# One loop per compute engine for all eight rounds, first round included, and whole-quad transfers at both ends of a gathered two-step residual matmul

## The chip, the cores and the metric

The kernel runs on one core of one Trainium2 chip. The metric is the device time of the program in microseconds (us), the median of several runs. TensorE has two clock levels, 1.2 and 2.4 GHz; the profile gives the granted one as a share of full speed (1.00 or 0.50).

## What is computed

```
x  = x + einsum('bct,bcd->bdt', x, W0[i_b])            # i_b = itok_B_1_198[b], 200 matrices of 128x128
x  = x + einsum('bct,bcd->bdt', x, W1[j_b]) + bias[j_b] # j_b = itok_B_0_7[b], 8 matrices of 128x128
# x: 128 batches b, 128 channels c, 1024 points t, float32
```

Both steps are linear in x, so the kernel forms one 128x128 matrix per batch and applies it once: with J = I + W1[j_b], the matrix is M = W0[i_b] J + J, and the output of the batch is M^T x + bias.

## The kernel before

x and out lie in memory as 32 quads of four batches (128 channels x 4 batches x 1024 points, 2 MB each). The ring `xy` in SBUF holds eight pairs of batches (slots 0 to 7), that is four quads; results are written over x in the same slot and stored from there. A round is one turn of the ring, 16 batches, and there are eight rounds.

For each batch the 64 KB matrix of W0 is loaded into its own place in `w0_home`. A batch whose index already occurred earlier uses the place of the first batch with that index (its home) and its load is skipped by a condition; homes are worked out on the chip by DVE and PE at the start (L353 to L367) from the 128 index words. Round 0 can't know them yet, so its 16 matrices are loaded without a condition and read from `w0_home` in place.

Per pair of batches (slot s):

- POOL: `pick` (L231) waits for the W0 matrices of the slot, reads two words per batch (home and j) from `pick_words`, and copies W0 to `w0_pick` and J to `j_pick`. Before that it waits until the quad that held the slot in the round before has been stored (L276). In round 0 `pick_first` (L248) copies J alone.
- PE: `product` (L281) makes W0 J of both batches in PSUM; `results` (L295) makes M^T x of one batch, as two halves of 512 points. The program order puts `product` of the next pair between the two batches of this pair, in every pair, also across the border between two rounds: the loop over rounds (L330) begins with the last pair of the round before. Round 0 stands unrolled ahead of the loop (L321 to L329), the last pair behind it.
- DVE: `sum_m` (L370) adds J to the product and gives M; `left` (L378) adds the bias to the left half and writes it to `xy`. Seven rounds are a loop, the eighth is written out.
- ACT: `right` (L400) does the right half. Seven rounds loop, one is written out.

SP issues every transfer but three, in program order. At the start: W1 with bias, both pairs of quad 0 (1 MB each), then for each quad its four W0 loads and the x load of the next quad (L176 to L184). Then three unrolled stretches, and a loop over rounds 1 to 6 (L203): for each quad the four W0 loads of the next quad, the store of the quad three back, and, once that slot's former contents are stored, the x load of this quad. SP reads index and condition of the W0 loads from `load_words`, two words per batch, in one read of eight words (L123).

The end (L211 to L227): the last quad of x is loaded as one pair (1 MB) and four pieces of 256 KB, each with a semaphore of its own; its second pair is stored as four pieces, two from SP (L225) and two from ACT (L421), each issued as soon as its half has been written.

```
            for k in range(PAIR):
                for h in range(2):
                    sp.dma_start(xy[:, LAST, k, half(h)], x[NQ - 1, :, QB - PAIR + k, half(h)])\
                      .then_inc(last_x_loaded[2 * k + h], 16)
```

Of the kernel before, what the change touches and what calls it, by code (L numbers as in the profile page):

```python
# [11 lines left out]
def conditioned_residual_kernel(nc, x, cond, w0_t, w1_bias, out):  # L12
# [12 lines left out]
    B = NQ * QB  # L25
# [16 lines left out]
    assert QUADS == 4 and QUAD == 2 and PAIRS % RING == 0 and HALF <= 512 and RING % MB == 0 and ROUND_B % YB == 0  # L42

    with ExitStack() as ctx:
# [16 lines left out]
        load_words = sb("load_words", [1, B, 2], I32)  # L61
        cond_words = sb("cond_words", [1, 2, B], I32)
        pick_words = sb("pick_words", [1, B, 2], I32)
# [21 lines left out]
        pair_loaded = [sem(f"pair_loaded{s}") for s in range(QUAD)]  # L85
# [3 lines left out]
        last_x_loaded = [sem(f"last_x_loaded{n}") for n in range(2 * PAIR)]  # L89
        last_stored = sem("last_stored")  # L90
# [25 lines left out]

        block = ctx.enter_context(nc.Block())

        @block.sync
        def _(sp):  # L120
            def words_of(words):

                return nc.values_load_multi_w_load_instructions(  # L123
                    words, engines=(mybir.EngineType.SP,), min_val=0, max_val=N0 - 1,
                    skip_runtime_bounds_check_because="the reference indexes a table of N0 rows with each cond word, "
                                                      "and each word of need is 0 or 1")[1]
# [6 lines left out]
            def load_w0_first(q):  # L133
                words = words_of(cond_words[0:1, 0, q * QB:(q + 1) * QB])
                for k in range(QB):
                    load_one(q * QB + k, q * QUAD + k // PAIR, words[k], None)

            def load_w0(r, s, pairs=1):

                for n in range(s, s + pairs):  # L140
                    sp.wait_ge(w0_loaded[n], r * (PAIR * 16))
                b = r * ROUND_B + s * PAIR
                words = words_of(load_words[0:1, bass.ds(b, pairs * PAIR), :].rearrange("o b f -> o (b f)"))
                for k in range(pairs * PAIR):
                    load_one(b + k, s + k // PAIR, words[2 * k], words[2 * k + 1])
# [7 lines left out]
            def wait_out(r, s):  # L153
                for k in range(PAIR):
                    b = s * PAIR + k
                    sp.wait_ge(left_out[b % YB], r * (ROUND_B // YB) + (b // YB + 1))  # L156
                    sp.wait_ge(right_out[b % YB], r * (ROUND_B // YB) + (b // YB + 1))
# [29 lines left out]
            sp.wait_ge(home_ready, 4)  # L187
# [39 lines left out]
            sp.wait_ge(last_stored, 2 * PAIR * 16)  # L227

        @block.gpsimd
        def _(pool):  # L230
            def pick(r, s):  # L231


                pool.wait_ge(w0_loaded[s], r * (PAIR * 16) + PAIR * 16)
                _, words = nc.values_load_multi_w_load_instructions(
                    pick_words[0:1, bass.ds(r * ROUND_B + s * PAIR, PAIR), :].rearrange("o b f -> o (b f)"),
                    engines=(mybir.EngineType.Pool,),
                    skip_runtime_bounds_check_because="each word is checked against its own range below")
                for k in range(PAIR):
                    home = nc.s_assert_within(words[2 * k], 0, B - 1)  # L240
                    i = nc.s_assert_within(words[2 * k + 1], 0, N1 - 1)
                    nc.gpsimd.tensor_copy(w0_pick[:, s, k, :],  # L242
                                          w0_home[:, bass.ds(home, 1), :].rearrange("k b c -> k (b c)"))
                    last = nc.gpsimd.tensor_copy(  # L244
                        j_pick[:, s, k, :], j_all[:, bass.ds(i, 1), :].rearrange("c n d -> c (n d)"))
                last.then_inc(picked, 1)

            def pick_first(s):  # L248


                _, words = nc.values_load_multi_w_load_instructions(
                    cond_words[0:1, 1, s * PAIR:(s + 1) * PAIR], engines=(mybir.EngineType.Pool,),
                    skip_runtime_bounds_check_because="each word is checked against its own range below")
                for k in range(PAIR):
                    i = nc.s_assert_within(words[k], 0, N1 - 1)
                    last = nc.gpsimd.tensor_copy(  # L256
                        j_pick[:, s, k, :], j_all[:, bass.ds(i, 1), :].rearrange("c n d -> c (n d)"))
                last.then_inc(picked, 1)

            nc.gpsimd.memset(ones[:], 1.0).then_inc(ones_ready, 1)  # L260
# [8 lines left out]
            for s in range(RING):  # L269
                pick_first(s)  # L270

            pool.wait_ge(home_ready, 4)
            with pool.Fori(1, ROUNDS) as r:
                for s in range(RING):

                    pool.wait_ge(stored[s // QUAD], stored_once(r, s // QUAD))  # L276
                    pick(r, s)

        @block.tensor
        def _(pe):  # L280
            def product(r, s, first=False):  # L281

                pe.wait_ge(picked, r * RING + (s + 1))
                if first:
                    pe.wait_ge(w0_loaded[s], PAIR * 16)
                if not first or s >= MB:

                    pe.wait_ge(m_ready[s % MB], r * (RING // MB) + s // MB)
                for k in range(PAIR):
                    w0_of_k = w0_home[:, s * PAIR + k, :] if first else w0_pick[:, s, k, :]  # L290
                    last = nc.tensor.matmul(m_ps[:, s % MB, k * D:(k + 1) * D], w0_of_k,  # L291
                                            j_pick[:, s, k, 0:D], start=True, stop=True)
                last.then_inc(product_ready, 1)

            def results(r, s, k, first=False, last=False):  # L295

                b = s * PAIR + k
                if k == 0:
                    if first and s < QUAD:
                        pe.wait_ge(pair_loaded[s], 16)  # L300
                    elif not last:
                        pe.wait_ge(x_loaded[s // QUAD], r * 16 + (16 if s >= QUAD else 0))
                    pe.wait_ge(m_ready[s % MB], r * (RING // MB) + (s // MB + 1))
                for h in range(2):
                    if last:
                        pe.wait_ge(last_x_loaded[2 * k + h], 16)
                    if not first or b >= YB:

                        pe.wait_ge((left_out, right_out)[h][b % YB], r * (ROUND_B // YB) + b // YB)
# [11 lines left out]
            product(0, 0, first=True)  # L321
# [16 lines left out]
            for k in range(PAIR):  # L338
                results(ROUNDS - 1, LAST, k, last=True)

        @block.vector
        def _(dve):

            dve.wait_ge(cond_loaded, 16)
            nc.vector.tensor_copy(cond0_row[:], cond_words[:, 0, :]).then_inc(cond0_row_ready, 1)  # L345
            dve.wait_ge(w1_loaded, 16)
            dve.wait_ge(eye_ready, 1)
            nc.vector.tensor_tensor(j_all[:, :, 0:D], j_all[:, :, 0:D],  # L348
                                    eye[:].rearrange("c (o d) -> c o d", o=1).to_broadcast([C, N1, D]), ALU.add)\
              .then_inc(j_ready, 1)  # L350
# [11 lines left out]
            nc.vector.tensor_copy(load_words[:, :, 0], cond_words[:, 0, :]).then_inc(home_ready, 1)  # L362
# [87 lines left out]
```

## Time and profile before

| | |
|---|---|
| median of 3 runs | 342.62 us (342.51 to 342.78) |
| profiled execution: own time | 343.0 us |
| profiled execution: span, first to last instruction | 341.2 us |
| PE busy | 272.9 us (80%) |
| DVE, ACT, POOL busy | 126.3, 97.0, 65.8 us |
| HBM read, written | 76.03 MB, 67.11 MB |
| mean granted clock | 0.952 |

Busy time is the sum of an engine's instructions; a busy share of PE isn't PE at its peak. DMA share in the stretches below is the mean over the core's 16 DMA engines, so 0.06 is one engine of 16 at work; it can read a few hundredths over 1. "To landing" is the time from a transfer's issue to the last of its completion signals.

### The profile page before, as it was taken

The page shows a single profiled execution, that of the slowest core. Times are in us where ns is not written, and L with a number is a line of the kernel's source. Part 1 is how long each engine was busy: PE and PEld are TensorE (multiplying, and loading weights), DVE is VectorE, ACT ScalarE, POOL GpSimd, SP SyncE. Part 2 cuts the span into 40 slices and gives each one's busy share as a digit, 9 for nine tenths or more (in the row PEclk, how much of TensorE's full clock was granted, in tenths as well). Part 3 has the DMA queues.
Part 4 walks back from the last instruction along what each step waited for, and adds up shares of the span by engine and source line. Part 5 has one row for each costly group of instructions (what it writes and reads, how often), then busy time and mean ns, then how long its engine had stood idle before and what let it go on. Part 6 is the DMA issues. An engine that isn't in the chain of part 4 may idle for free.

```text
span 341.2 us, 4867 instructions
## 1 busy us (share of the span) xinstructions
PE 272.9 (80%) x774; PEld 131.8 (39%) x774; DVE 126.3 (37%) x202; ACT 97.0 (28%) x135; POOL 65.8 (19%) x249
## 2 busy tenths in 40 slices
PE   1799997678777798786997977889697987978980
PEld 1355443334333354343443433444343443434430
DVE  3145543343333334243442433434243432424440
ACT  1033352232322224132241324313143321323330
POOL 2400311131122211222111222121222111222000
PEclk9999999999999979799897999979799997989996
DMA  7999999999999999999999999999999999999993
GB/s 304 417 409 396 422 430 419 413 423 421 432 434 423 426 422 414 431 424 423 427 427 423 431 430 426 427 421 426 433 426 430 427 429 426 425 426 424 413 387 137
DMA packets 24058, 140.80 MB, mean 413 GB/s; under 512 B 2673, under 2 KB 14322, under 8 KB 15474
## 3 DMA queue, kind: packets, MB, share of 16 engines
q1 hardware_dynamic: 23760, 140.20, 98.7%
q10 hardware_dynamic: 290, 0.53, 0.4%
q14 instruction: 7, 0.06, 0.0%
q8 instruction: 1, 0.02, 0.0%
HBM read 76.03 MB, written 67.11 MB: 419 GB/s over the span
## 4 chain that ended last, share of the span: by engine, by line
DMA 61%; SPq 16%; PE 13%; issue 7%; ACT 0%; DVE 0%; DVEq 0%
DMA out<-xy 54%; PE y_ps L310 11%; SPq L129 9%; SPq L123 5%; DMA xy<-x 4%; DMA w_home<-w_t 2%; PE m_ps L291 2%; SPq L148 2%; ACT xy L406 0%; SPq L162 0%; SPq L151 0%; SPq L203 0%; SPq L156 0%; PE home_ps L324 0%; SPq L176 0%
## 5 line engine op out<-in xcount | busy, mean ns | idle before, releaser
L310 PE MATMUL y_ps<-xy,m_sb 128*128 128x512 f32 x512 | 251.4, 627 | 49.2 <-DMA xy<-x 48.2
L310 PEld LDWEIGHTS y_ps<-xy,m_sb 128*128 128x128 f32 x512 | 94.6, 200 | 155.1 <-issue 155.1
L406 ACT ACTIVATE xy<-y_ps,j_pick 128x512 f32<-128x512 f32 x128 | 88.0, 687 | 227.4 <-PE y_ps L310 227.4
L382 DVE TENSOR_SCALAR xy<-y_ps,j_pick 128x512 f32<-128x512 f32 x128 | 96.1, 751 | 147.9 <-PE y_ps L310 147.9
L242 POOL COPY w_pick<-w_home 128x128 f32 x112 | 33.2, 296 | 238.3 <-issue 238.3
L291 PEld LDWEIGHTS m_ps<-j_pick,w_pick 128*128 128x128 f32 x224 | 35.7, 200 | 30.2 <-issue 29.7
L374 DVE TENSOR_TENSOR m_sb<-m_ps,j_pick 128x256 f32<-128x256 f32 x64 | 27.2, 425 | 47.7 <-PE m_ps L291 46.1
L291 PE MATMUL m_ps<-j_pick,w_pick 128*128 128x128 f32 x224 | 34.9, 279 | 0.0
L244 POOL COPY j_pick<-j_all 128x129 f32 x112 | 33.4, 298 | 0.1
L291 PE MATMUL m_ps<-j_pick,w_home 128*128 128x128 f32 x32 | 5.9, 315 | 6.6 <-DMA w_home<-w_t 6.6
L406 ACT ACT_TABLE_LOAD x7 | 9.0, 1283 | 7.5 <-POOL j_pick L256 7.4
L291 PEld LDWEIGHTS m_ps<-j_pick,w_home 128*128 128x128 f32 x32 | 5.7, 225 | 10.6 <-POOL j_pick L256 7.2
L256 POOL COPY j_pick<-j_all 128x129 f32 x16 | 4.8, 298 | 9.9 <-issue 9.5
L316 PE MATMUL cond_ps<-cond_row,ones 1*128 1x128 f32 x2 | 0.8, 482 | 2.4 <-DVE cond_row L345 2.4
L365 DVE TENSOR_TENSOR load_words<-home_ps,batch_less_b 1x128 int32<-1x128 f32 x1 | 0.3, 280 | 5.0 <-PE home_ps L324 5.0
L348 DVE TENSOR_TENSOR j_all<-j_all,eye 128x1024 f32<-128x1024 f32 x1 | 1.2, 1226 | 1.9 <-DMA j_all<-w_bias 1.9
L316 PEld LDWEIGHTS cond_ps<-cond_row,ones 1*128 1x128 f32 x2 | 0.5, 305 | 2.4 <-issue 2.4
L345 DVE CAST cond_row<-cond_words 1x128 f32<-1x128 int32 x1 | 0.2, 215 | 2.1 <-DMA cond_words<-cond 2.1
L324 PE MATMUL home_ps<-eye,home_less_b 128*1 128x128 f32 x2 | 0.6, 394 | 0.0
L317 PEld LDWEIGHTS cond_ps<-ones,cond_row 1*128 1x128 f32 x2 | 0.5, 328 | 0.0
L317 PE MATMUL cond_ps<-ones,cond_row 1*128 1x1 f32 x2 | 0.4, 277 | 0.0
L355 DVE TENSOR_SCALAR same<-cond_ps,cond_col 128x128 f32<-128x128 f32 x1 | 0.4, 351 | 0.0
(16 smaller groups left out, 2.8 us busy)
## 6 DMA issues: line engine op xcount, KB each, us to landing
xy<-x SPq DMA_DIRECT2D x30, 2048.0 KB, 15.1
out<-xy SPq DMA_DIRECT2D x29, 2048.0 KB, 15.0
w_home<-w_t SPq DMA_DIRECT2D x128, 64.0 KB
out<-xy SPq DMA_DIRECT2D x5, 1024.0 KB, 9.7
xy<-x SPq DMA_DIRECT2D x3, 1024.0 KB, 7.7
xy<-x SPq DMA_DIRECT2D x4, 256.0 KB, 13.4
j_all<-w_bias SPq DMA_DIRECT2D x1, 516.0 KB, 3.4
out<-xy SPq DMA_DIRECT2D x2, 256.0 KB, 4.7
```

Of the source, the lines that this page charges most:

```text
L123: return nc.values_load_multi_w_load_instructions(words, engines=(mybir.EngineType.SP,), min_val=0, max_val=N0 - 1, skip_runtime_bounds_ch ...
L129: sp.dma_start(w0_home[:, bass.ds(b, 1), :].rearrange("k b c -> k (b c)"), w0_t[bass.ds(i, 1), :, :].rearrange("n k c -> (n k) c"), cond=n ...
L148: sp.dma_start(slots(q), quad_of(x, r, q)).then_inc(x_loaded[q], 16)
L242: nc.gpsimd.tensor_copy(w0_pick[:, s, k, :], w0_home[:, bass.ds(home, 1), :].rearrange("k b c -> k (b c)"))
L244: last = nc.gpsimd.tensor_copy(j_pick[:, s, k, :], j_all[:, bass.ds(i, 1), :].rearrange("c n d -> c (n d)"))
L256: last = nc.gpsimd.tensor_copy(j_pick[:, s, k, :], j_all[:, bass.ds(i, 1), :].rearrange("c n d -> c (n d)"))
L291: last = nc.tensor.matmul(m_ps[:, s % MB, k * D:(k + 1) * D], w0_of_k, j_pick[:, s, k, 0:D], start=True, stop=True)
L310: nc.tensor.matmul(y_ps[:, b % YB, h, :], m_sb[:, s, k, :], xy[:, s, k, half(h)], start=True, stop=True).then_inc(y_ready, 1)
L316: nc.tensor.matmul(cond0_ps[:, 0:B], ones[:], cond0_row[:], start=True, stop=True)
L374: nc.vector.tensor_tensor(m_sb[:, s, :, :], m_ps[:, s % MB, 0:PAIR * D].rearrange("c (k d) -> c k d", k=PAIR), j_pick[:, s, :, 0:D], ALU.a ...
L382: nc.vector.tensor_scalar(xy[:, s, k, half(0)], y_ps[:, b % YB, 0, :], j_pick[:, s, k, D:D + 1], None, ALU.add).then_inc(left_out[b % YB], 1)
L406: nc.scalar.activation(xy[:, s, k, half(1)], y_ps[:, b % YB, 1, :], ACT.Identity, bias=j_pick[:, s, k, D:D + 1]).then_inc(right_out[b % YB ...
```

## The change

What it does:

- Each of PE, DVE, ACT and POOL runs one loop of eight rounds; nothing is unrolled before or behind it. At the border of two rounds `product` of slot 0 now follows the last batch of the round before, it is no longer put between that pair's two batches.
- Round 0 is like the others: POOL picks W0 and J for it too, and so waits for the homes (`home_ready`) before its first copy. POOL works by quads (`pick_quad`): one read of four j words and one of four home words, then for each pair two J copies, the wait for W0, two W0 copies. It waits for the results of the round before in these slots, not for their store.
- `load_words` and `pick_words`, two words per batch, are gone. SP reads the index words as they came (`cond_words`) and the condition from `need_words`, two reads of four words; every word has its range stated where it is read, so the separate range instructions go.
- DVE makes the homes before it adds I to W1; `ones` is set by DVE, not POOL. `left_out` and `right_out` begin at 8, so that the first round waits by the same formula.
- Start: pair 1 of quad 0 is issued behind the four W0 loads of quad 0, and each later quad's x load ahead of its W0 loads.
- End: the last x quad is one load of 2 MB, and the second pair of the last quad is stored as one transfer of 1 MB by SP once all four halves are written. SP alone waits for the stores.
- The instructions of all engines take 55 KB, not 85.

```diff
@@ SP @@
-            for s in range(QUAD):
-                load_pair(0, s, pair_loaded[s])
+            load_pair(0, 0, x_loaded[0])
             sp.wait_ge(cond_loaded, 16)
-            for q in range(QUADS):
+            load_w0_first(0)
+            load_pair(0, 1, x_loaded[0])
+            for q in range(1, QUADS):
+                load_quad(0, q)
                 load_w0_first(q)
-                if q < QUADS - 1:
-                    load_quad(0, q + 1)
...
             store_quad(ROUNDS - 1, 0)
-            sp.wait_ge(stored[QUADS - 1], stored_once(ROUNDS - 1, QUADS - 1))
-            load_pair(NQ - 1, LAST - 1, x_loaded[QUADS - 1])
-            for k in range(PAIR):
-                for h in range(2):
-                    sp.dma_start(xy[:, LAST, k, half(h)], x[NQ - 1, :, QB - PAIR + k, half(h)])\
-                      .then_inc(last_x_loaded[2 * k + h], 16)
+            load_quad_again(ROUNDS - 1, QUADS - 1)
             for q in range(1, QUADS - 1):
                 store_quad(ROUNDS - 1, q)
             store_pair(ROUNDS - 1, LAST - 1)
-            for k in range(PAIR):
...
-                b = LAST * PAIR + k
-                sp.wait_ge(left_out[b % YB], (ROUNDS - 1) * (ROUND_B // YB) + b // YB + 1)
-                sp.dma_start(out[NQ - 1, :, QB - PAIR + k, half(0)], xy[:, LAST, k, half(0)]).then_inc(last_stored, 16)
...
+            store_pair(ROUNDS - 1, LAST)
...
@@ POOL @@
+            def pick_quad(r, q):
...
+                pool.wait_ge(left_out[YB - 1], pick_free(r, q * QUAD + QUAD - 1))
+                pool.wait_ge(right_out[YB - 1], pick_free(r, q * QUAD + QUAD - 1))
+                for p in range(QUAD):
+                    s = q * QUAD + p
+                    for k in range(PAIR):
+                        nc.gpsimd.tensor_copy(
+                            j_pick[:, s, k, :],
+                            j_all[:, bass.ds(j_of[p * PAIR + k], 1), :].rearrange("c n d -> c (n d)"))
...
+                    pool.wait_ge(w0_loaded[s], r * (PAIR * 16) + PAIR * 16)
...
-            for s in range(RING):
-                pick_first(s)
...
-            pool.wait_ge(home_ready, 4)
-            with pool.Fori(1, ROUNDS) as r:
-                for s in range(RING):
...
-                    pool.wait_ge(stored[s // QUAD], stored_once(r, s // QUAD))
-                    pick(r, s)
+            pool.wait_ge(home_ready, 2)
+            with pool.Fori(0, ROUNDS) as r:
+                for q in range(QUADS):
+                    pick_quad(r, q)
@@ PE @@
-            product(0, 0, first=True)
...
-            for s in range(1, RING):
-                results(0, s - 1, 0, first=True)
-                product(0, s, first=True)
-                results(0, s - 1, 1, first=True)
-            with pe.Fori(1, ROUNDS) as r:
-                results(r - 1, LAST, 0)
+            with pe.Fori(0, ROUNDS) as r:
                 product(r, 0)
-                results(r - 1, LAST, 1)
-                for s in range(1, RING):
-                    results(r, s - 1, 0)
-                    product(r, s)
-                    results(r, s - 1, 1)
-            for k in range(PAIR):
-                results(ROUNDS - 1, LAST, k, last=True)
+                for s in range(RING):
+                    results(r, s, 0)
+                    if s < LAST:
+                        product(r, s + 1)
+                    results(r, s, 1)
@@ ACT @@
-            for k in range(PAIR):
-                b = LAST * PAIR + k
-                right(ROUNDS - 1, LAST, k)
-                act.wait_ge(right_out[b % YB], (ROUNDS - 1) * (ROUND_B // YB) + b // YB + 1)
-                act.dma_start(out[NQ - 1, :, QB - PAIR + k, half(1)], xy[:, LAST, k, half(1)]).then_inc(last_stored, 16)
```

How it moves instructions, at the places that the prediction speaks of. First PE's first instructions, before (x is `xy`, the matrix M is `m_sb`):

```order
L317 MATMUL cond_ps<-ones,cond_row 128x1
L291 MATMUL m_ps<-j_pick,w_home 128x128 [waits w0_loaded0,picked]
L291 MATMUL m_ps<-j_pick,w_home 128x128
L324 MATMUL home_ps<-eye,home_less_b 1x128 [waits home_step,eye_ready]
L310 MATMUL y_ps<-xy,m_sb 128x512 [waits m_ready0,pair_loaded0]
```

and with the change:

```order
L315 MATMUL cond_ps<-ones,cond_row 128x1
L321 MATMUL home_ps<-eye,home_less_b 1x128 [waits home_step,eye_ready]
L323 UNCONDITIONAL_BRANCH
L323 ISA
L294 MATMUL m_ps<-j_pick,w_pick 128x128 [waits picked]
L294 MATMUL m_ps<-j_pick,w_pick 128x128
```

The homes' last step on PE (`home_ps`) stood behind the first product and its wait for W0; now it stands ahead of it.

Second, the transfers that SP issues at the end, before:

```order
L162 DMA out<-xy 128x4096 [waits left_out1,right_out1,right_out0,left_out0]
L151 DMA xy<-x 128x2048 [waits stored3]
L216 DMA xy<-x 128x512 x4
L162 DMA out<-xy 128x4096 [waits left_out1,right_out1,right_out0,left_out0] x2
L166 DMA out<-xy 128x2048 [waits left_out1,right_out1,right_out0,left_out0]
L225 DMA out<-xy 128x512 [waits left_out0]
L225 DMA out<-xy 128x512 [waits left_out1]
L44 UNCONDITIONAL_BRANCH [waits last_stored]
```

and with the change:

```order
L185 DMA out<-xy 128x4096 [waits left_out1,right_out1,right_out0,left_out0]
L171 DMA xy<-x 128x4096 [waits stored3]
L185 DMA out<-xy 128x4096 [waits left_out1,right_out1,right_out0,left_out0] x2
L189 DMA out<-xy 128x2048 [waits left_out1,right_out1,right_out0,left_out0] x2
L45 UNCONDITIONAL_BRANCH [waits stored2,stored3,stored1,stored0]
```

The last quad comes in as one transfer and its second pair goes out as one.

## Rows read from the trace of the kernel before

**Rows 1.** The profile page: span, and DMA share in 40 slices.
```profile
span 341.2 us, 4867 instructions
...
DMA  7999999999999999999999999999999999999993
```

**Rows 2.** Busy time by stretch: start and length, engines, clock, DMA share, GB/s.
```profile
core 0: us, PE busy (x) PEld busy (x) DVE busy (x) ACT busy (x) POOL busy (x), PEclk, DMA share, GB/s
...
240.00:300.00 60.00, 49.91 (x139) 23.56 (x138) 22.53 (x36) 17.10 (x24) 12.85 (x48) 0.94 1.01 428
...
324.00:325.00 1.00, 1.00 (x4) 0.45 (x3) 0.29 (x1) 0.09 (x1) 0.00 (x0) 1.00 0.22 90
325.00:330.00 5.00, 5.00 (x16) 2.47 (x15) 2.38 (x4) 1.87 (x3) 0.00 (x0) 1.00 1.01 428
330.00:335.00 5.00, 1.12 (x3) 0.19 (x1) 0.75 (x1) 0.88 (x2) 0.00 (x0) 1.00 1.00 397
336.00:337.00 1.00, 0.00 (x0) 0.00 (x0) 0.00 (x0) 0.00 (x0) 0.00 (x0) 0.50 0.12 47
...
339.00:340.00 1.00, 0.00 (x0) 0.00 (x0) 0.00 (x0) 0.00 (x0) 0.00 (x0) 0.50 0.06 25
```

**Rows 3.** Who waited for whom, all engines, then SP's queue: us in total, times, longest.
```profile
PE y_ps L310 <- DMA xy<-x: 48.2, 27, 3.0
...
SPq L44 <- DMA out<-xy: 9.4, 1, 9.4
```

**Rows 4.** Transfers to landing: SP's L216, SP's last L225, ACT's last L421.
```profile
L216 SPq DMA_DIRECT2D xy<-x x4: 521/660/770, 310.7 to 312.7; - x4
...
DMA to landing us min/median/max: 13.3/13.4/13.4
...
L225 SPq DMA_DIRECT2D out<-xy x1: 332/332/332, 331.1 to 331.1; - x1
...
DMA to landing us min/median/max: 4.5/4.5/4.5
...
L421 ACTq DMA_DIRECT2D out<-xy x1: 338/338/338, 331.9 to 331.9; - x1
...
DMA to landing us min/median/max: 8.9/8.9/8.9
```

**Rows 5.** Timeline of the last quads: start us, us, engine, line, what, idle before.
```profile
304.83 3.62 PE L310 MATMUL y_ps<-xy,m_sb 128*128 128x512 f32 x4 [2.43 <-DMA xy<-x]
...
323.57 1.95 PE L310 MATMUL y_ps<-xy,m_sb 128*128 128x512 f32 x4 [0.21 <-DMA xy<-x]
...
331.16 0.69 ACT L406 ACTIVATE xy<-y_ps,j_pick 128x512 f32<-128x512 f32 x1 [0.97 <-PE y_ps L310]
```

**Rows 6.** Stretch of the slow matmuls of rows 5, columns as in rows 2.
```profile
304.80:308.20 3.40, 3.37 (x4) 1.52 (x5) 0.75 (x1) 0.00 (x0) 0.00 (x0) 0.50 1.02 439
```

**Rows 7.** Timeline of the start.
```profile
2.88 2.16 SPq L129 DMA_DIRECT2D w_home<-w_t  x4
...
5.30 0.15 DVE L353 COPY cond_col<-cond_ps 128x1 f32<-128x1 f32 x1
...
6.65 0.66 POOL L256 COPY j_pick<-j_all 128x129 f32 x2 [4.80 <-issue]
...
10.04 1.19 PE L291 MATMUL m_ps<-j_pick,w_home 128*128 128x128 f32 x4 [6.61 <-DMA w_home<-w_t]
...
12.73 3.75 PE L310 MATMUL y_ps<-xy,m_sb 128*128 128x512 f32 x4 [0.99 <-DVE m_sb L374]
```

**Rows 8.** Timeline of PE across a border of two rounds.
```profile
80.08 3.60 PE L310 MATMUL y_ps<-xy,m_sb 128*128 128x512 f32 x8
```

**Rows 9.** DMA queues: packets, MB, share of 16 engines.
```profile
q1 hardware_dynamic: 23760, 140.20, 98.7%
q10 hardware_dynamic: 290, 0.53, 0.4%
q14 instruction: 7, 0.06, 0.0%
```

More of the change, by code:

```diff
@@ L120, in _, with words_of, index_words @@
         def _(sp):
-            def words_of(words):
+            def words_of(words, last, why):
                 return nc.values_load_multi_w_load_instructions(
-                    words, engines=(mybir.EngineType.SP,), min_val=0, max_val=N0 - 1,
-                    skip_runtime_bounds_check_because="the reference indexes a table of N0 rows with each cond word, "
-                                                      "and each word of need is 0 or 1")[1]
+                    words, engines=(mybir.EngineType.SP,), min_val=0, max_val=last,
+                    skip_runtime_bounds_check_because=why)[1]
+            def index_words(b):
+                return words_of(cond_words[0:1, 0, b], N0 - 1,
+                                "the reference indexes a table of N0 rows with each of these cond words")
             def load_one(b, s, i, needed):
@@ L229, in _ @@
+            sp.wait_ge(stored[QUADS - 1], stored_once(ROUNDS, QUADS - 1) + 16)
         @block.gpsimd
         def _(pool):
[L231 to L238, printed above, removed]
-                for k in range(PAIR):
[L240 to L253, printed above, removed]
-                for k in range(PAIR):
[L255 to L258, printed above, removed]
@@ L260, in _, with words_of @@
-            nc.gpsimd.memset(ones[:], 1.0).then_inc(ones_ready, 1)
+            def words_of(words, last, why):
+                return nc.values_load_multi_w_load_instructions(
+                    words, engines=(mybir.EngineType.Pool,), min_val=0, max_val=last,
+                    skip_runtime_bounds_check_because=why)[1]
+            def pick_quad(r, q):
+                b = bass.ds(r * ROUND_B + q * QB, QB)
+                j_of = words_of(cond_words[0:1, 1, b], N1 - 1,
+                                "the reference indexes a table of N1 rows with each of these cond words")
+                home_of = words_of(home_words[0:1, b], B - 1,
+                                   "a home is the number of the first batch with the same w0, so it is below B")
+                pool.wait_ge(left_out[YB - 1], pick_free(r, q * QUAD + QUAD - 1))
[7 more added lines that the diff above has]
+                    pool.wait_ge(w0_loaded[s], r * (PAIR * 16) + PAIR * 16)
+                    for k in range(PAIR):
+                        last = nc.gpsimd.tensor_copy(
+                            w0_pick[:, s, k, :],
+                            w0_home[:, bass.ds(home_of[p * PAIR + k], 1), :].rearrange("k b c -> k (b c)"))
+                    last.then_inc(picked, 1)
@@ L279, in _, with product @@
         @block.tensor
         def _(pe):
-            def product(r, s, first=False):
+            def product(r, s):
                 pe.wait_ge(picked, r * RING + (s + 1))
[L284 to L288, printed above, removed]
                 for k in range(PAIR):
-                    w0_of_k = w0_home[:, s * PAIR + k, :] if first else w0_pick[:, s, k, :]
-                    last = nc.tensor.matmul(m_ps[:, s % MB, k * D:(k + 1) * D], w0_of_k,
+                    last = nc.tensor.matmul(m_ps[:, s % MB, k * D:(k + 1) * D], w0_pick[:, s, k, :],
@@ L292, in product, with results @@
                                             j_pick[:, s, k, 0:D], start=True, stop=True)
                 last.then_inc(product_ready, 1)
-            def results(r, s, k, first=False, last=False):
+            def results(r, s, k):
                 b = s * PAIR + k
                 if k == 0:
[L299 to L303, printed above, removed]
+                    if s % QUAD == 0:
+                        pe.wait_ge(x_loaded[s // QUAD], x_loaded_once(r, s // QUAD))
+                    pe.wait_ge(m_ready[s % MB], m_made(r, s))
@@ L304, in results @@
                 for h in range(2):
[L305 to L309, printed above, removed]
+                    pe.wait_ge((left_out, right_out)[h][b % YB], y_free(r, b))
                     nc.tensor.matmul(y_ps[:, b % YB, h, :], m_sb[:, s, k, :], xy[:, s, k, half(h)],
```

80 lines of the change are left out of this document (41 added, 39 removed).

## The prediction

> **What bounds the kernel now.** I read the page's row of the DMA share first, since 140 MB in 341 us is a lot for one core: it stands at nine tenths or more from the second slice to the last but one [rows 1]. The stretches say the same in numbers: from 240 to 300 us the 16 DMA engines are busy all the time (share 1.01) and move 428 GB/s, while PE, the busiest compute engine, works 49.91 of 60 us [rows 2]. PE waited 27 times for x, 48.2 us in all, 1.8 us a time [rows 3]. So the transfers set the pace in the middle, and a change on a compute engine there counts only if it makes the DMA engines run dry.
>
> Then the end, in three views. The stretches show a hole from 324 to 325 us (share 0.22): SP's store of quad 2 was issued at 324.2, behind the results of that quad, and nearly everything ahead of it had gone. From 325 the share is full again until 335, and then falls to 0.12 and at last to 0.06, one engine of 16, at 25 GB/s [rows 2]. The landings tell who that is: SP's last piece, issued at 331.1, landed 4.5 us later at 335.6; ACT's last piece, issued at 331.9, landed 8.9 us later, at 340.8 [rows 4], and SP ended its wait for it then [rows 3]. The two are alike in size, so one DMA engine is some 5 us behind the other 15, and the span ends with its queue, not with the last result (ACT done at 331.85) [rows 5].
>
> That queue can be added up. The last piece of x, issued at 312.7, was complete after 13.4 us, at 326.1 [rows 4]. Behind it lie three stores' worth of results: quads 1 and 2 (2 MB each) and the two pairs of quad 3 (1 MB each), 6.29 million bytes, 0.393 million per engine. At 428/16 = 26.75 GB/s per engine [rows 2] that is 14.7 us, and 326.1 + 14.7 = **340.8**, just the landing. The late engine has thus no hole at all, not even at 324 to 325; it is the resource that bounds the kernel to its last microsecond.
>
> The Trainium skill (DMA: Bandwidth & Descriptors, Latency and other measured facts) says that two of the 16 engines are usually slower, and guesses at rings that only software-made descriptors use. Here all data go through hardware queues [rows 9] and an engine is late all the same, so the guess doesn't carry to this case. By that guess the end would be set by the 15 others; that is a rival below.
>
> **The change, part by part.** The sum is made against the profiled execution, 343.0 us of its own time (span 341.2, 1.8 around it); the median of the runs is 342.62, 0.4 below.
>
> *The end.* The same bytes are left when x is complete: the load of quad 3 is 2 MB either way, and it ends in the same place of the queue, so all of it is there at about 326.0. What changes is who may begin. Before, PE began on pair 0 of this quad at 323.57 [rows 5], when the first megabyte had come; now it must wait for 2 MB, 2.4 us more. Its work on the two pairs took from 323.57 to 331.16, 7.6 us, so now 326.1 + 7.6 = 333.7. But PE will have been idle for some 2.7 us ahead of it (it finished quad 2 about 0.2 before 323.57). At 304.83, behind an idle time of 2.43 us, four matmuls took 3.62 us [rows 5] at a granted clock of 0.50, that is 1.2 GHz [rows 6], where the four at 323.57, behind 0.21 us of idle time, took 1.95 [rows 5]. I add the difference, 1.7 us: 335.4, with ACT's 0.7 us 336.1, and SP issues the last megabyte at **336.2**. From issue to the first bytes I take 1.0 us, from the hole: issued at 324.2, share full again from 325 [rows 2]. The data start at 337.2. The late engine reaches this megabyte at 340.8 less 1/16 MB at 26.75 GB/s (2.45 us), at **338.4**. So the store is there 1.2 us before its turn, and costs nothing. The 15 others are idle in between but need only 337.2 + 2.45 = 339.7, also before 340.8. Without this cover (no late engine) the compute tail would show. In return the pieces' rows of 2 KB become rows of 8 and 16 KB. No row prices that; the sum above fits to 0.1 us with one rate for both, so the gain lies between 0 and 0.3, and I take 0.1. SP's last waits are four where it waited for one semaphore and ACT for four: 0 to 0.4 us, taken as 0.1 since all but one are long met.
>
> *The start.* SP issues pair 1 behind four W0 loads, which took 2.16 us [rows 7], so at about 4.7 us and not at 1.7. The 0.5 MB of W1 and 1 MB of pair 0, issued before, last to about 6 us, and the four W0 loads stand between: the engines don't run dry. Bounds 0 and 0.5 us, taken 0. The homes come sooner: DVE's first step of them no longer stands behind the addition to W1 (`cond_col` at 5.30), PE's last no longer behind the wait for W0 (10.04) [rows 7]. They should be ready at 6.5 and not at 12.3; POOL adds two reads of words and two W0 copies per pair (a pair of copies is 0.66 us), so the first product comes at 9.5 to 10 and the first `y_ps` at about 11, not 12.73 [rows 7]. That lets stores be issued up to 1.7 us earlier, into a queue that is full in this time [rows 1]: worth nothing, bounds 0 and -1.7.
>
> *The middle.* SP reads 4 + 4 words for 8, and drops the range instructions; it issues the same transfers in the same order. POOL's picks wait for less (results, not stores). PE's product of slot 0 now stands alone between two rounds, as does DVE's sum: product 0.6 and sum 0.4 us, no longer overlapped, 1.2 us with the way between, eight times. It falls into the time in which PE waits for the next x, 1.8 us a time [rows 3], so 0. If that cover were gone, it would be 9 us. In the last quad there is no such border.
>
> *The code.* 30 KB less to fetch. The trace shows 7 packets, 0.06 MB, of instruction fetch in the span [rows 9], on the same DMA engines. All 30 KB on the late engine would be 30 KB at 26.75 GB/s, 1.1 us; spread over 16, under 0.1. I take 0.1.
>
> **Sum:** -0.1 (rows) + 0.1 (waits) + 0 + 0 + 0 - 0.1 (code) = -0.1 us: 342.9 for a profiled execution, and **342.5** against the median 342.62. No change, then: under 0.2% (0.7 us), which is about the least that a measurement of this kernel can tell from none.
>
> **The rivals.**
> 1. *The last store comes too late (slower).* Place: PE's last quad. It decides from 337.4 on: an issue later than that misses the late engine's turn at 338.4, and each microsecond more is one on the end. For it: only 1.2 us of margin, and a quad wholly at 1.2 GHz costs 16 matmuls and 2 products at twice the time, some 14 to 15 us for 7.6, so issue at 341.5 and an end of 345, about +4. Against it: the low stretch at 304.8 ended within 3.4 us, four matmuls [rows 5, 6]. Half way is 344.5. Chance 0.12.
> 2. *Stalls at the loops' ends (slower).* The Trainium skill (Runtime: NRT & Kernel Launch, Instruction fetch mechanics) says that a taken branch whose target is outside the two fetched pages stalls the engine for a DMA fetch, and advises full unrolling; that speaks against this change. As a mechanism here: one stall on each of PE, DVE, ACT and POOL at every border of rounds, in a DMA queue some 10 us deep for a newly issued packet (transfers land 13 us after issue [rows 4]), 10 us a round in the worst case, 2 us of it hidden. Against it: PE crossed such a border in eight matmuls that took 3.60 us without a gap [rows 8]. Should it show once or twice only, where a larger body no longer fits, the time would be 344 to 346. Chance 0.04.
> 3. *The fetches lay on the late engine (faster).* Then up to 1.1 us go: 341.5. For it: something makes one engine late, and fetches are small transfers to few engines. Against: 7 packets in 341 us explain at most 2 us of 5. Chance 0.14.
> 4. *The late engine isn't late after the change,* as the guess on software rings would have it. Then the end is 339.7 + 0.4, about 1 us less: 341.5. Every full run of before speaks against it. Chance 0.03.
> 5. *The earlier first result is passed on,* so that the change's new order of the start does pay: 342.6 - 1.7 = 340.9. The full DMA share speaks against it. Chance 0.02.
>
> **How the numbers follow.** The forecast (within 0.7 us of 342.62) has 0.65; rivals 3 to 5 make faster 0.19, rivals 1 and 2 slower 0.16. The range takes in rival 3, the lower bounds of the code and of the rows (-1.1, -0.3) and above the bounds of waits and start (+0.4, +0.5) and the first third of rival 1: 341.3 to 344.0.
>
> **What the profile after should show.** DMA share full to about 331, then a partial hole up to 333 (the 15 engines wait for the store of the next to last pair), another near 336, and one engine alone to 340.7. PE's first matmul of the last quad at 326, slow; last ACT at 335.4 to 336; SP's last store issued near 336 and landed near 340.7. First `y_ps` at 11 us. No idle time on PE for x shorter than 1 us at a round's border. Wrong would be: the last store landing 3.5 us after its issue with 16 engines alike (then compute set the end), or a hole in the DMA share at a border of rounds.

## The result: 0.4% slower, and the profile after

| | before | changed |
|---|---|---|
| median | 342.62 us (7 runs, 342.15 to 343.08) | 343.98 us (7 runs, 342.56 to 344.91) |
| ratio, with its 95% interval | | 1.0038 [1.0021, 1.0056] |
| profiled execution, own time | 343.0 us | 342.56 us |

The forecast was 342.5 us: no change, to within 0.2%. The measured median is 1.36 us above the kernel before, and the interval excludes both no difference and 0.2%. The runs also spread more than before: 2.35 us between the fastest and the slowest, where the kernel before shows 0.93. (Over the whole study 4 of the 94 executions of the kernel before took over 343.5 us, one of them 346.28, and 23 of the 31 with pair 1 behind four W0 loads.) And the profiled execution is the fastest of the seven. A reader who compares two pages alone would call this change slightly faster. One profile isn't enough here.

The whole of it looks like the one before: DMA share and end [rows 1], PE's wait for x and SP's last wait [rows 3]:

```profile
span 340.8 us, 4236 instructions
...
DMA  8999999999999999999999999999999999999975
```

```profile
PE y_ps L308 <- DMA xy<-x: 45.2, 25, 3.0
...
SPq L243 <- DMA out<-xy: 4.9, 1, 4.9
```

The end, by stretches with the columns of [rows 2]: the partial hole that was 324 to 325 us is now longer, then the share is nearly full to 337, 0.36 from 337 to 338, and then one engine alone is at work to 340:

```profile
325.00:330.00 5.00, 4.90 (x15) 2.27 (x14) 2.44 (x4) 1.51 (x3) 0.00 (x0) 1.00 0.69 292
330.00:335.00 5.00, 3.26 (x8) 1.14 (x6) 1.50 (x2) 1.92 (x3) 0.00 (x0) 1.00 0.93 388
...
339.00:340.00 1.00, 0.00 (x0) 0.00 (x0) 0.00 (x0) 0.00 (x0) 0.00 (x0) 0.50 0.04 16
```

The last store, SP's L189, with its landing (it answers to the last pieces in [rows 4]), and PE's and ACT's last work [rows 5]:

```profile
L189 SPq DMA_DIRECT2D out<-xy x1: 332/332/332, 334.1 to 334.1; - x1
...
DMA to landing us min/median/max: 6.2/6.2/6.2
```

```profile
315.87 3.56 PE L308 MATMUL y_ps<-xy,m_sb 128*128 128x512 f32 x4 [2.59 <-DMA xy<-x]
...
327.94 5.32 PE L308 MATMUL y_ps<-xy,m_sb 128*128 128x512 f32 x12
```

A megabyte alone on 16 engines needs 1.0 + 2.45 us by the forecast's own rows; this one took 6.2, to 340.3. So here too the last store stood in the queue of one late engine, and the results were there in time. That reading holds in every profile of the study: the last landing of all came 14.8 to 15.4 us after the last piece of x was complete, whether the last store had been issued 6.0 us after that (the kernel before) or 8.6 (every kernel with the changed end). The forecast's sum for this queue was 14.7.

The start [rows 7] is where something new stands. SP's queue and then PE:

```profile
1.21 0.43 SPq L174 DMA_DIRECT2D xy<-x  x1
2.80 1.97 SPq L150 DMA_DIRECT2D w_home<-w_t  x4
4.82 0.43 SPq L174 DMA_DIRECT2D xy<-x  x1
```

```profile
8.85 1.22 PE L294 MATMUL m_ps<-j_pick,w_pick 128*128 128x128 f32 x4 [3.42 <-POOL w_pick L270]
11.30 3.77 PE L308 MATMUL y_ps<-xy,m_sb 128*128 128x512 f32 x4 [1.23 <-DMA xy<-x]
```

The first result came at 11.3 us and not at 12.73, as forecast. But the stretch from 6 to 9 us moved less than before. First the kernel before, then the changed one:

```profile
6.00:9.00 3.00, 0.00 (x0) 0.00 (x0) 0.71 (x4) 1.28 (x1) 1.19 (x4) 1.00 0.99 401
```

```profile
6.00:9.00 3.00, 0.15 (x1) 0.15 (x1) 0.22 (x2) 0.11 (x1) 1.20 (x6) 1.00 1.06 352
```

49 GB/s less for 3 us are 0.15 MB, 0.3 us at 428 GB/s: little, but this is the fastest execution. The first experiment's profile shows what the others look like.

One correction to the list of the change further up: the sequence of the later x and W0 transfers at the start is the same in both kernels (W0 of quad 0, x of quad 1, W0 of quad 1, and so on). Only pair 1 moved, from ahead of the W0 loads of quad 0 to behind them.

### The profile page after: what moved, and what is told of

Its sections match the earlier page's. It is cut to its first block, busy times and chain, and to the rows that moved or that the text cites. A ratio compares the mean times of both kernels' runs of the same rounds, so it can differ in the third digit from the quotient of the medians.

```text
span 340.8 us, 4236 instructions
## 1 busy us (share of the span) xinstructions
PE 278.6 (82%) x774; PEld 135.8 (40%) x774; DVE 126.2 (37%) x201; ACT 98.2 (29%) x136; POOL 64.9 (19%) x264
## 4 chain that ended last, share of the span: by engine, by line
DMA 64%; SPq 18%; PE 11%; issue 5%; ACT 1%
DMA out<-xy 50%; DMA xy<-x 13%; SPq L150 10%; PE y_ps L308 10%; SPq L141 5%; SPq L171 2%; PE m_ps L294 1%; ACT xy L395 1%; DMA cond_words<-cond 0%; SPq L185 0%; SPq L179 0%; SPq L226 0%; SPq L174 0%; SPq L180 0%; SPq L189 0%
## 5 line engine op out<-in xcount | busy, mean ns | idle before, releaser
L270 POOL COPY w_pick<-w_home 128x128 f32 x128 | 33.9, 293 | 204.7 <-DMA w_home<-w_t 204.7
L294 PEld LDWEIGHTS m_ps<-j_pick,w_pick 128*128 128x128 f32 x256 | 44.1, 217 | 40.0 <-issue 33.7
L294 PE MATMUL m_ps<-j_pick,w_pick 128*128 128x128 f32 x256 | 43.8, 299 | 3.4 <-POOL w_pick L270 3.4
L264 POOL COPY j_pick<-j_all 128x129 f32 x128 | 34.0, 295 | 36.7 <-issue 23.5
## 6 DMA issues: line engine op xcount, KB each, us to landing
out<-xy SPq DMA_DIRECT2D x29, 2048.0 KB, 15.4
```

The source lines that it names most:

```text
L264: nc.gpsimd.tensor_copy(j_pick[:, s, k, :], j_all[:, bass.ds(j_of[p * PAIR + k], 1), :].rearrange("c n d -> c (n d)"))
L270: last = nc.gpsimd.tensor_copy(w0_pick[:, s, k, :], w0_home[:, bass.ds(home_of[p * PAIR + k], 1), :].rearrange("k b c -> k (b c)"))
```

## Experiments

Two theories were set against each other. **T**, the forecast's first rival in its widest form: the coarser end leaves too little cover. **S**: at the start the DMA engines run short, because pair 1 is queued too late, and time lost by the late engine can't be won back. A third possibility, the loops and picks, had to be told apart from both.

### 1. The changed kernel again

No edit. 

> The changed kernel once more. Its first runs spread from 342.56 to 344.91 us, where the kernel before spread 0.9 us. Theory T (the tail: the last whole-quad load and whole-pair store leave too little cover, and which run is slow is decided by where TensorE's low-clock stretch falls): +1.0 to +1.6 us over the kernel before, spread of 2 us, and a profile in which the last store's issue or the late DMA engine's landing of it is late. Theory S (the start: pair 1 behind the W0 loads): the same time, but the excess is there by 30 us.

Measured: 343.64 us, 12 runs (342.64 to 344.61), ratio 1.0022 [1.0008, 1.0036]. The profiled execution took 344.14. Its start:

```profile
6.00:9.00 3.00, 0.21 (x1) 0.21 (x2) 0.15 (x1) 0.17 (x1) 1.26 (x6) 1.00 0.87 255
```

255 GB/s where the kernel before has 401: 0.44 MB less, 1.0 us at full rate, and a DMA share of 0.87, so engines stood idle and others moved slowly. SP issued pair 1 at 4.7, and this transfer landed 7.1 us later:

```profile
L174 SPq DMA_DIRECT2D xy<-x x1: 424/424/424, 4.7 to 4.7; - x1
...
DMA to landing us min/median/max: 7.1/7.1/7.1
```

At 11.8, then, where pair 1 landed at 9.4 in the kernel before (issued at 1.7, 7.7 us to landing).

The trace also lists every packet with its size, and the size tells what it belongs to: 512 bytes is a row of W0, 8 KB a row of a pair. In the kernel before, pair 1's first packet starts at 6.12 us, as pair 0's last does at 6.08, and takes 0.31 us like the others; the W0 rows come at 8.46 to 9.82. Here the W0 rows come at 5.93 to 7.38. Pair 1's first packet starts at 6.97, 2.2 us after its issue, its first 16 packets take 0.60 us each on the average, and its last packet starts at 11.2 and not at 8.8. So the loss has two parts, engines without work and slow first packets. The end of this execution had wide holes for 15 engines (332 to 333: share 0.09; 335.5 to 336.5: 0.07), yet the last store still landed 6.2 us after its issue at 335.7:

```profile
339.50:340.50 1.00, 0.00 (x0) 0.00 (x0) 0.00 (x0) 0.00 (x0) 0.00 (x0) 0.50 0.06 25
```

One engine alone, to 341.9. This speaks for S and against T, but it is one execution.

### 2. Pair 1 back in its place

```diff
             load_pair(0, 0, x_loaded[0])
+            load_pair(0, 1, x_loaded[0])
             sp.wait_ge(cond_loaded, 16)
-            load_w0_first(0)
-            load_pair(0, 1, x_loaded[0])
-            for q in range(1, QUADS):
-                load_quad(0, q)
+            for q in range(QUADS):
                 load_w0_first(q)
+                if q < QUADS - 1:
+                    load_quad(0, q + 1)
```

> The changed kernel with the start's transfer order of the kernel before. Theory T: no effect, +1.0 to +1.6 us over the kernel before. Theory S: within 0.4 us of the kernel before.

Measured: 342.64 us, 12 runs, 0.9991 [0.9970, 1.0011]. And again:

> The changed kernel with pair 1 issued right behind pair 0, once more, on another chip or day: within 0.3 us of the kernel before (0.9991 the first time).

Measured: 343.03 us against 342.80, 1.0011 [0.9998, 1.0024]. From 6 to 9 us the first profile has 391 GB/s, the second 396:

```profile
6.00:9.00 3.00, 0.35 (x2) 0.00 (x0) 1.13 (x3) 0.00 (x0) 0.28 (x2) 1.00 0.97 391
```

Taken together no difference from the kernel before; both intervals hold 1. The loss is gone with this one edit, as S says; T expected no effect. But the first profile is of an execution of 344.79 us, the slowest of its twelve. Its start is full, and it lost its time elsewhere: from 240 to 300 us it moved 412 GB/s, where the kernel before moved 428. Why isn't known. A slow execution is thus no proof of a bad start; the medians have to carry the argument.

### 3. The changed end alone, on the kernel before

```diff
             store_quad(ROUNDS - 1, 0)
-            sp.wait_ge(stored[QUADS - 1], stored_once(ROUNDS - 1, QUADS - 1))
-            load_pair(NQ - 1, LAST - 1, x_loaded[QUADS - 1])
-            for k in range(PAIR):
-                for h in range(2):
-                    sp.dma_start(xy[:, LAST, k, half(h)], x[NQ - 1, :, QB - PAIR + k, half(h)])\
-                      .then_inc(last_x_loaded[2 * k + h], 16)
+            load_quad_again(ROUNDS - 1, QUADS - 1)
...
             store_pair(ROUNDS - 1, LAST - 1)
-            for k in range(PAIR):
...
+            store_pair(ROUNDS - 1, LAST)
```

(PE's waits for the pieces and ACT's two transfers go with it.) 

> The kernel before, with the changed end alone (last quad of x in one load, its second pair stored whole). Theory T: +1.0 to +1.6 us over the kernel before and its wide spread. Theory S, or any cause in the loops or picks: within 0.4 us of the kernel before.

Measured: 342.33 us, 11 runs (341.94 to 342.92), 0.9992 [0.9983, 1.0001]. T falls: the coarse end costs nothing, by its sign it gains a little. Repeated:

> The kernel before with the changed end alone, once more, since it may be the fastest of all: 0.1 to 0.5 us faster than the kernel before (0.9992 the first time), or no difference if that was chance.

342.41 us against 342.80, 0.9992 [0.9981, 1.0002]. The same ratio twice, each time with an interval that ends at 1: likely 0.3 us faster than both kernels, and the fastest version of the study, but not beyond doubt.

### 4. The changed kernel with the end of the kernel before

The reverse of edit 3; PE's and ACT's last round is written out for it. 

> The changed kernel with the end of the kernel before (pair and four pieces in, four pieces out; only the last round is written out on PE and ACT for it). Theory T: within 0.4 us of the kernel before, with its narrow spread. Theory S, or any cause in the loops or picks: +1.0 to +1.6 us.

Measured: 344.12 us, 5 runs (343.66 to 344.82), 1.0042 [1.0029, 1.0055]. The loss stays with the old end in place, so T falls here as well. Its profile shows 244 GB/s from 6 to 9 us:

```profile
6.00:9.00 3.00, 0.31 (x2) 0.00 (x0) 1.10 (x3) 0.00 (x0) 0.31 (x2) 1.00 0.79 244
```

### 5. The late pair 1 alone, on the kernel before

```diff
-            for s in range(QUAD):
-                load_pair(0, s, pair_loaded[s])
+            load_pair(0, 0, pair_loaded[0])
             sp.wait_ge(cond_loaded, 16)
             for q in range(QUADS):
                 load_w0_first(q)
+                if q == 0:
+                    load_pair(0, 1, pair_loaded[1])
```

> The kernel before, with pair 1 of quad 0 issued behind the four W0 loads of quad 0, and nothing else. Theory S (at the start the 16 DMA engines run short between 6 and 9 us because SP has too little queued, and the late DMA engine that ends the span never gets that time back): +0.7 to +1.5 us over the kernel before, 240 to 360 GB/s from 6 to 9 us where the kernel before has 401. Theory L (it is the loops and picks that make the start of round 0 sensitive, pair 1 matters only there): within 0.3 us.

Measured: 343.70 us, 7 runs (342.47 to 344.27), against 342.77, 1.0029 [1.0018, 1.0041]. One line's place on the kernel before makes +0.93 us and the wide spread. The profile is again of its fastest execution, 342.47:

```profile
6.00:9.00 3.00, 1.23 (x5) 1.00 (x6) 1.09 (x5) 1.18 (x1) 1.17 (x4) 1.00 0.99 314
```

How can this execution be fast with such a start? The traces show 16 completion signals for each x load, as many as there are DMA engines, and I read them as one for each engine's share. Take the x load of quad 1 in the eighth round. Its eighth signal then stands for a typical engine, its 16th for the late one. In the kernel before, in experiment 3 twice, and in three other versions with pair 1 early (the second run of experiment 2, the first version of experiment 6, and experiment 7) the eighth came at 299.2 to 299.6 us. (In the first run of experiment 2, with its slow stretch just before, it came at 301.6.) In the four profiles with pair 1 behind four W0 loads it came at 300.0 to 300.4. What a typical engine loses at the start is still missing 290 us later. The 16th, though, came 3.9 us (this execution) to 7.0 us (experiment 4) after the eighth. So how late the late engine is varies by more than the loss does, and here it hid the loss.

This run also rules out a rival. The changed kernel has one semaphore for both pairs of quad 0, so that PE's first result waits for pair 1. Here PE waits for each pair by itself, its first `y_ps` comes at 10.50 us, and the loss is there all the same.

### 6. How late is too late

Three places for pair 1 in the changed kernel, and one other way to fill the queue. First ahead of the four W0 loads, but behind SP's wait for the index words:

> The changed kernel with pair 1 issued behind the wait for the index words but ahead of the four W0 loads, at 2.1 to 3 us. Theory S (the queue must hold more than pair 0 when the small W0 loads begin): 390 us or more GB/s from 6 to 9 us and within 0.3 us of the kernel before. If pair 1 must be issued before that wait: between the kernel before and the changed one, +0.3 to +0.7 us.

Measured: 342.63 us against 342.80, 0.9998 [0.9989, 1.0007]; 389 GB/s from 6 to 9 us. No loss. In the changed kernel's place, four loads later, it is 1.0022 to 1.0038. Between them, behind two W0 loads (the call behind the four goes):

```diff
                 for k in range(QB):
                     load_one(q * QB + k, q * QUAD + k // PAIR, i_of[k], None)
+                    if q == 0 and k == PAIR - 1:
+                        load_pair(0, 1, x_loaded[0])
```

> The changed kernel, with pair 1 issued behind two W0 loads and not four, about 1 us earlier. Theory S: the gap closes wholly or nearly, 0 to +0.5 us over the kernel before, 370 to 400 GB/s from 6 to 9 us. Theory P (it isn't the queue's depth but that small rows stand ahead of a large transfer in the queue): still +0.7 to +1.1 us.

Measured: 343.17 us against 342.77, 1.0010 [1.0000, 1.0020], within theory S's 0 to 0.5 us. But the profiled execution has 273 GB/s from 6 to 9 us, not the 370 to 400 expected, and took 343.97, the slowest of its eleven. In it the first W0 load was issued at 3.68, not at 2.8:

```profile
3.68 0.91 SPq L150 DMA_DIRECT2D w_home<-w_t  x2
```

Pair 1 followed at 4.64. The index words had come about 0.9 us later, as also in the first profile of experiment 2 and in that of experiment 4 (first W0 load at 3.72 and 3.68 us). Where pair 1 stands ahead of the wait for them the rate from 6 to 9 us doesn't suffer: experiment 2's profile kept 391 GB/s. Behind it, every delay of the index words delays pair 1 as well. That is likely one source of the spread; how often it occurs isn't known from a profile each.

Then behind eight W0 loads:

```diff
             load_w0_first(0)
+            load_w0_first(1)
             load_pair(0, 1, x_loaded[0])
-            for q in range(1, QUADS):
+            load_quad(0, 1)
+            for q in range(2, QUADS):
                 load_quad(0, q)
                 load_w0_first(q)
```

> The changed kernel, with pair 1 and then quad 1 issued behind eight W0 loads, 2.5 to 3 us later still. Theory S: the time lost grows by that delay, +3 to +4.5 us over the kernel before, under 150 GB/s in some microsecond before 10 us. Theory P, or a cause behind the start: +0.7 to +1.5 us.

Measured: 343.96 us, 5 runs (343.57 to 345.30), 1.0037 [1.0024, 1.0051], +1.2 us. None at the wait, +0.4 behind two, +0.9 to +1.5 behind four, +1.2 behind eight: the loss grows up to four loads, and behind eight it can't be told from four. Theory S had expected 3 to 4.5 us, so its size was wrong. The +1.2 lies in the band that was written down for theory P (0.7 to 1.5 us), by which it isn't the depth of the queue that counts but that small rows stand ahead of a large transfer. The profile shows 205 GB/s from 6 to 9 us, and 146 in the last of the three (S had expected under 150 in some microsecond), but no stretch of nothing. In this profile, of an execution of 345.30 us, a typical engine is later than in any other: its signal for quad 1 in the eighth round came at 301.6. So a growth with the delay isn't excluded, only one to 3 us in the median:

```profile
2.74 4.41 SPq L150 DMA_DIRECT2D w_home<-w_t  x8
```

```profile
6.00:9.00 3.00, 0.21 (x1) 0.21 (x2) 0.15 (x1) 0.16 (x1) 1.26 (x6) 1.00 0.82 205
```

SP issues one 64 KB load in 0.55 us there (eight in 4.41), so it supplies about 120 GB/s of W0 loads while pair 1 waits (an estimate from these two numbers), and those bytes needn't be moved later. A queue of small transfers isn't empty, it is thin; that would account for the small growth, though no run tested it by itself.

Last, the queue made deep in another way: quad 1 (2 MB) right behind pair 0, with pair 1 where the change has it.

```diff
             load_pair(0, 0, x_loaded[0])
+            load_quad(0, 1)
             sp.wait_ge(cond_loaded, 16)
             load_w0_first(0)
             load_pair(0, 1, x_loaded[0])
-            for q in range(1, QUADS):
+            load_w0_first(1)
+            for q in range(2, QUADS):
                 load_quad(0, q)
                 load_w0_first(q)
```

> The changed kernel, with quad 1 (2 MB) issued right behind pair 0; pair 1 stays behind the four W0 loads. Theory S: the queue is deep again, within 0.3 us of the kernel before, 390 to 430 GB/s from 6 to 9 us, though W0 of quad 0 lands at about 12 us and the first y_ps comes at 13 to 14 us. Theory P: +0.7 to +1.1 us. If an early first result mattered: slower by the 2 to 3 us that it comes later.

Measured: 343.17 us, 11 runs (342.89 to 344.05), 1.0012 [1.0003, 1.0021]. The early gap is closed, with pair 1 still behind four W0 loads. For the rate from 6 to 9 us it is therefore the depth of the queue that counts, as S says:

```profile
6.00:9.00 3.00, 0.00 (x0) 0.00 (x0) 0.15 (x1) 0.00 (x0) 0.53 (x2) 1.00 1.05 445
...
30.00:60.00 30.00, 29.33 (x92) 14.88 (x92) 14.32 (x23) 11.78 (x17) 6.40 (x26) 1.00 1.02 404
```

But not all of the time came back: +0.4 us lies between S (within 0.3) and P (0.7 to 1.1), so the time alone doesn't decide between them. The first `y_ps` was at 15.48 us, and from 30 to 60 us the engines moved 404 GB/s, where the kernel before moved 423: 0.57 MB less, 1.3 us. The engines were busy all the while (share 1.02), so the same bytes took the engines longer; why, and whether that follows from the later first result, stays open. The spread is narrower again (1.16 us, 1 of 11 over 343.5), which fits: here the queue is deep when the index words come.

### 7. The loops and picks alone

The changed kernel with start and end as before. 

> The changed kernel with both its start and its end as before: what is left of the change is the loops, the picks of round 0, the picks by quads and the words. If these cost nothing, as forecast: within 0.3 us of the kernel before. If the border of two rounds or the later picks cost something: slower by over 0.5 us.

Measured: 342.94 us, 12 runs (342.49 to 343.62), against 342.80, 1.0005 [0.9995, 1.0016]. No difference that can be measured: one loop of eight rounds on DVE and POOL, the picks of round 0 and the border of two rounds come out at 0.1 us together. For the old end PE and ACT have their last round written out here. The versions that loop all eight rounds on every engine and have pair 1 early (experiment 2, and the first of experiment 6) show no cost either: 0.9991, 1.0011 and 0.9998.

The parts against the kernel before, each alone and by its ratio: loops, picks and words +0.2 us, end -0.3, late pair 1 +1.0. Their sum, +0.9, lies within both intervals of the changed kernel: +0.3 to +1.2 us in experiment 1 and +0.7 to +1.9 in its first seven runs.

## Why the prediction was wrong, by its steps

**The bound was right.** In every profile of the study one DMA engine lands last and alone, 14.8 to 15.4 us after the last of x, where the forecast's queue sum has 14.7. A bound of this kind has no slack in which a loss at the start could be absorbed: the typical engines still miss it at 300 us (experiment 5), and the median has it at the end. In a single execution the late engine's own lateness, which varies by some 3 us, can hide it or add to it. The forecast had named this bound ("the resource that bounds the kernel to its last microsecond") and then didn't use it for the start.

**The step that failed is "The start".** It read: the 0.5 MB of W1 and 1 MB of pair 0, issued before, last to about 6 us, and the four W0 loads stand between: the engines don't run dry; bounds 0 and 0.5 us, taken 0. Three things were wrong with it.

- It compared issue with issue. Pair 1 was issued at 4.7 to 4.8, before the engines had worked off pair 0 at 6 to 7 us. But its data came later than the forecast's own 1.0 us from issue to first bytes, the figure it had from the end of the kernel. In the profile of experiment 1 its first packet started 2.2 us after issue, and its first 16 took 0.60 us each and not 0.31. The rate recovered only behind 9 us (412 GB/s from 9 to 12), and pair 1 landed 7.1 us after issue. Why the first packets are late and slow there isn't settled.
- It counted the W0 loads as cover by their number, not their bytes. Four are 0.26 MB, 0.6 us at full rate. Their 512-byte packets did take longer, 1.45 us in the profile of experiment 1 (5.93 to 7.38), but at a low rate: from 6.5 to 7.5 us the core moved 227 GB/s.
- It left out that pair 1 now stands behind a wait, for the index words, whose time varies by 0.9 us. What this adds wasn't measured by itself: behind the wait alone (first version of experiment 6) there was no loss.

The term, taken as 0, was worth +0.9 us ([1.0018, 1.0041] of 343 us: +0.6 to +1.4), against an upper bound of 0.5 in the forecast. No other term that was measured was off by as much as 0.4.

**The end** was right. Forecast: no cost, a gain of 0.1 (0 to 0.3) from larger rows; measured 0.3 us gain, with intervals that reach 0. What makes this gain, if there is one, no run shows. The sequence differed in detail: PE's stretch at 1.2 GHz fell into quad 2 (315.87: four matmuls in 3.56 us, granted clock 0.54 from 315.8 to 319.5) and not into quad 3, so quad 2's store went out at 326.4 and not at 324.2, and the last store at 334.1 and not at 336.2. In experiment 1 it was 335.7, in time too; there PE stood idle for 1.81 us ahead of the last quad, and its four matmuls still took only 1.98 us, so the 1.7 us that the forecast added for a low clock didn't come at the last quad in either execution.

**The middle, the picks and the code** were right at 0: experiment 7 has +0.1. Rival 2 (stalls at the loops' ends) is ruled out by it, and the Trainium skill's rule (Runtime: NRT & Kernel Launch, Instruction fetch mechanics) that a branch outside the fetched pages stalls the engine shows no price here: the interval of experiment 7 ends at +0.55 us for the loops and picks together. Rival 3 (the fetches lie on the late engine) isn't borne out either: the versions with the short code and an early pair 1 gained nothing that can be measured (0.9991, 1.0011, 0.9998). Rival 5 (the earlier first result is passed on) has nothing for it: 1.4 us earlier at the start, no gain. Rival 4 didn't occur. Rival 1, the only slower one with a real chance, fell with experiments 3 and 4. That a rival on the slower side was named was luck: its mechanism was the wrong one.

**The chances** were wrong in that the side "slower" had two places, the end (0.12) and the borders of the loops (0.04), and none at the start. The list of rivals came from the part of the kernel that had been looked at longest. The range, 341.3 to 344.0, does hold 343.98, by a hair, and that too is luck: its topmost part had been taken in for rival 1.

What stays open: why one DMA engine is late, and why its lateness differs from execution to execution; why the first packets of pair 1 are late and slow behind W0 loads; why the median loss behind eight W0 loads is no larger than behind four; why 30 to 60 us is slower with quad 1 first.

## What to carry to other kernels

Where the transfers bound a kernel from end to end, the first 10 us count as much as the last: put the large transfers that need nothing ahead of any wait and of small transfers, and check the depth of the queue in bytes at the moment when the small ones begin. A wait in front of a transfer passes on that wait's variation. A wider spread can be a sign of lost cover, but count the late executions in a long series before using it: here it was 23 of 31 against 4 of 94, while the spread from fastest to slowest of the kernel before also reached 4.2 us. And when one profile contradicts the median, profile again before explaining anything.

## What was new about the hardware

- With eight 64 KB loads queued one behind the other (128 rows of 512 bytes each), SP took 4.41 us to issue them, 0.55 us each, and from 6 to 9 us the core moved 205 GB/s. With 2 MB more queued ahead of the first four it moved 445 GB/s in the same stretch.
- One DMA engine of 16 finished alone in every execution profiled. The last 1 MB store took 6.2 us to land, in an execution with its issue at 334.1 as in one with 335.7, though 15 engines were free. The lateness grows over the span: in the kernel before, the 16th completion signal of quad 1's x load came 0.4 us after the eighth in the first round and 5.4 us after it in the eighth round.
- The share of the DMA engines was full again 1 us after the issue in the hole at 324 us [rows 2]. Behind four 64 KB loads at the start, the first packet of a 1 MB load started 2.2 us after issue, and its first 16 packets of 8 KB took 0.60 us each, where 0.31 us is usual in that load (experiment 1).
